# Vision tower on one core: the routed stage loads a place's expert weights in parts, without the rows that nobody reads

## What is computed

```python
def _L1_ffn_ref(hidden_states, Wg, W1, b1, W2, b2):
    x = hidden_states.reshape(-1, d)
    logits = x @ Wg
    probs = jax.nn.softmax(logits, axis=-1)
    gate = jnp.max(probs, axis=-1)
    expert_idx = jnp.argmax(probs, axis=-1)
    h = jax.nn.silu(jnp.einsum('td,edf->etf', x, W1) + b1[:, None, :])
    y = jnp.einsum('etf,efd->etd', h, W2) + b2[:, None, :]
    combine = jax.nn.one_hot(expert_idx, e, dtype=x.dtype) * gate[:, None]
    out = jnp.einsum('te,etd->td', combine, y)
```

## Time and profile before

| | |
|---|---|
| median of three executions | 3292.92 us (3288.41 to 3302.89) |
| the profiled execution's own time | 3293.8 us |
| its span | 3292.0 us |
| mean granted TensorE clock | 0.927 |
| TensorE busy | 2926.8 us (89%) |
| VectorE busy | 2119.5 us (64%) |
| loads of `w_e` | 20 of 1344 KB, median 6.4 us from issue to landing |

### The profile page before, as it was taken

How to read it: one execution, slowest core, us unless ns; L and a number is a source line. 1 busy time by engine, 2 the same in 40 slices (tenths; PEclk the granted TensorE clock), 3 DMA queues, 4 the chain that set the end, 5 groups by cost and what they waited for, 6 DMA issues and landing times. The chain is left out here.

```text
span 3292.0 us, 56595 instructions
## 1 busy us (share of the span) xinstructions
PE 2926.8 (89%) x19969; PEld 2685.5 (82%) x19969; DVE 2119.5 (64%) x5372; ACT 1109.3 (34%) x2263; POOL 608.1 (18%) x734
## 2 busy tenths in 40 slices
PE   7979999999999999999969896978969799695677
PEld 6759999999999999999968886656858699583567
DVE  2657777777777677777757773234466667785666
ACT  2433333333333233333233333114444333243333
POOL 1111221221221221221221110211223112120320
PEclk8989999999999999999989997998979889897788
DMA  3010000000000000000000000650000100000000
GB/s 128 1 51 18 35 34 34 34 18 33 34 34 34 34 17 34 34 34 34 0 36 2 1 2 5 229 195 3 1 10 18 51 18 1 10 2 3 13 18 16
DMA packets 19244, 107.77 MB, mean 33 GB/s; under 512 B 3861, under 2 KB 8869, under 8 KB 11178
## 3 DMA queue, kind: packets, MB, share of 16 engines
q1 hardware_dynamic: 17434, 101.81, 8.6%
q0 software_dynamic: 1584, 3.30, 0.3%
HBM read 100.50 MB, written 6.64 MB: 33 GB/s over the span
## 5 line engine op out<-in xcount | busy, mean ns | idle before, releaser
L766 ACT ACTIVATE hid<-bank,dat 128x384 f32<-128x384 f32 (+1 forms) x912 | 554.2, 608 | 1151.8 <-PE bank L484 1042.2
L735 PE MATMUL bank<-w,hid_hi 128*128 128x384 f32 x2964 | 848.8, 358 | 0.0
L737 PE MATMUL bank<-w,hid_lo 128*128 128x192 f32 x2964 | 742.0, 250 | 0.0
L737 PEld LDWEIGHTS bank<-w,hid_lo 128*128 128x128 f32 x2964 | 565.7, 191 | 1.7
L798 DVE TENSOR_TENSOR hid_lo<-hid,hid_hi 128x384 fp32r<-128x384 f32 (+1 forms) x912 | 539.8, 592 | 31.5
L735 PEld LDWEIGHTS bank<-w,hid_hi 128*128 128x128 f32 x2964 | 556.4, 188 | 1.8
L795 DVE CAST hid_hi<-hid 128x384 fp32r<-128x384 f32 (+1 forms) x912 | 341.0, 374 | 145.4 <-ACT hid L766 143.5
L484 PE MATMUL bank<-xa_hi,w_hi 128*128 128x384 f32 (+1 forms) x912 | 328.0, 360 | 8.6 <-DVEq L2018 8.6
L809 DVE SCALAR_TENSOR_TENSOR h_tok<-bank,gate,h_tok 128x192 f32<-128x192 f32 x416 | 173.2, 416 | 245.9 <-PE bank L737 240.9
L484 PE MATMUL bank<-xb,w_hi 128*128 128x384 f32 (+1 forms) x912 | 325.4, 357 | 0.0
L484 PE MATMUL bank<-xb,w_lo 128*128 128x384 f32 (+1 forms) x912 | 325.2, 357 | 0.0
(11 more groups left out here) (352 smaller groups left out, 4587.4 us busy)
## 6 DMA issues: line engine op xcount, KB each, us to landing
raw<-in_L_exp SPq DMA_DIRECT2D x36, 1344.0 KB, 5.7
w_e<-in_L_exp SPq DMA_DIRECT2D x20, 1344.0 KB, 6.4
pix<-in_pixels SPq DMA_DIRECT2D x6, 832.0 KB, 9.2
wp_raw<-in_L_att SPq DMA_DIRECT2D x1, 2880.0 KB, 9.9
raw<-in_L_mlp SPq DMA_DIRECT2D x2, 1344.0 KB, 5.9
route_rows<-in_rows_clear SPq DMA_DIRECT2D x1, 2000.0 KB, 22.2
x_in<-route_rows SPq DMA_DIRECT2D x5, 400.0 KB, 9.4
wp_raw<-in_L_att SPq DMA_DIRECT2D x2, 768.0 KB, 4.5
```

What stands on the lines that cost most here:

```text
L735: nc.tensor.matmul(o[:, 0:2 * D], hid_hi[k % 2][:, m, c], w2[j][:, m, :], start=m == 0, stop=False)
L737: ins = nc.tensor.matmul(o[:, 0:D], hid_lo[k % 2][:, m, c], w2[j][:, m, 0:D], start=False, stop=m == HC - 1)
L766: nc.scalar.activation(hid[(6 * k + m) % 3][:, 0:128 * nt], bank[4 + (6 * k + m) % 4][:, 0:128 * nt], func, bias=bias).then_inc(s["h_act"] ...
```

## The change

A place's load becomes three DMAs with two counters. The up part is 128 rows of 768 floats and 65 rows of 768 floats, both counted by `w_up_in`; the down part is 128 rows of 1152 floats, counted by `w_down_in`. Each part looks up the expert anew. From place 4 on the up part of a buffer is reloaded once `up` of the place before in it is done (`up_full`), the down part once `down` of that place is (`y_full`). `up` waits for 32 of `w_up_in`, `down` in addition for 16 of `w_down_in`.

```diff
-        w_e_in = [ctx.enter_context(nc.semaphore(f"w_e_in{j}")) for j in range(4)]
+        w_up_in = [ctx.enter_context(nc.semaphore(f"w_up_in{j}")) for j in range(4)]
+        w_down_in = [ctx.enter_context(nc.semaphore(f"w_down_in{j}")) for j in range(4)]
...
-                def weights(p):
+                def of_expert(p):
                     e = sp.value_load(place[0:1, p:p + 1], min_val=0, max_val=E - 1)
-                    sp.dma_start(w_e[p % 4][:, :], pack[bass.ds(e, 1)].rearrange("o p n -> p (o n)"))\
-                        .then_inc(w_e_in[p % 4], 16)
+                    return pack[bass.ds(e, 1)].rearrange("o p n -> p (o n)")
+
+                def up_weights(p):
+
+                    w, src = w_e[p % 4], of_expert(p)
+                    sp.dma_start(w[:, 0:HID], src[:, 0:HID]).then_inc(w_up_in[p % 4], 16)
+                    sp.dma_start(w[0:DB + 1, HID:2 * HID], src[0:DB + 1, HID:2 * HID]).then_inc(w_up_in[p % 4], 16)
+
+                def down_weights(p):
+                    w, src = w_e[p % 4], of_expert(p)
+                    sp.dma_start(w[:, 2 * HID:RAW], src[:, 2 * HID:RAW]).then_inc(w_down_in[p % 4], 16)
                 for p in range(3):
-                    weights(p)
+                    up_weights(p)
+                    down_weights(p)
...
                     if q == 0:
-                        weights(3)
+                        up_weights(3)
+                        down_weights(3)
+
                 for p in range(4, N):
+                    for ahead in range(p if p == 4 else p + 2, min(p + 3, N)):
+                        sp.wait_ge(route["up_full"], 2 * (ahead - 4) + 2)
+                        up_weights(ahead)
                     sp.wait_ge(route["y_full"], p - 3)
-                    weights(p)
+                    down_weights(p)
...
                 def up(p):
-                    pe.wait_ge(w_e_in[p % 4], 16 * (p // 4 + 1))
+                    pe.wait_ge(w_up_in[p % 4], 32 * (p // 4 + 1))
...
                 def down(p):
+                    pe.wait_ge(w_down_in[p % 4], 16 * (p // 4 + 1))
                     if p >= 1:
                         pe.wait_ge(route["y_kept"], p)
```

## The result

The changed kernel takes 3281.93 us (median of 15 executions, 3274.67 to 3290.34), the kernel before 3297.17 us (15 executions, 3288.41 to 3307.18) in the same measurement. The ratio is 0.9954, with a 95% interval of 0.9945 to 0.9964. That is 15.2 us; the prediction was a gain of 14.8 us and a ratio of 0.9955. The time lies inside the range of 3269 to 3290. The gain is clear of zero and, as forecast, a little under the 0.5% (16.5 us) that the prediction took as its bound for "faster".

The account below looks back on a forecast made before the run. It took TensorE and, behind it, the weight loads to bound the routed stretch. 15.95 us excess less 0.85 for the clock and 0.3 for small waits gave a 14.8 us gain: 3278.1 us, ratio 0.9955, range 3269 to 3290.

Parts of the forecast that it names:

- The sum: Routed stage: 15.95 less 0.85 for the clock and 0.3 for extra waits and the start, a gain of 14.8 us.
- the free pace: Step of TensorE's routed loop without a wait: 5.42 us, sixteen of them 86.72 us against 102.67 us.
- path: Time from a weight buffer's release to the landing of its next load; 6.87 us in the kernel before.
- cover: Time from a weight buffer's release until TensorE is ready to read it again; 5.64 us before, 19.1 us for up after.
- more than the sum: Rival: waits may be longer in some executions than in the profile, a gain of 18 to 22 us; chance 15%.
- all of it comes from one fact: Waits of `up` for `w_e` arise because its buffer is refilled only after `down(p-4)`; removal gains 15.95 us at most.
- Half clock: After the 2.72 us wait before `up(6)`, TensorE's lower clock cost 1.7 us; half counted as lost gain, 0.85 us.
- Fewer bytes: 63 of 128 rows of a place's second part not loaded, 14% fewer bytes; worth nothing beside the long cover.
- the forecast share: DMA engines' busy share in the routed stretch after the change: up to about 0.7.
- a sign against the prediction: Routed loop: SyncE issuing a down part over 3 us after its release would show the prediction wrong.
- The extra wait on TensorE: `down` waits for three semaphores in place of two: 0 for each of 20, at most 0.05 us each, 1 us in all.
- The slower rival: The 65-row load runs on too few DMA engines; if on one, 11.3 us a place, about 3370 us; chance 4%.

Follow-up runs that it names:

- the two orders: Kernel before with each place's load split into up and down DMAs with own semaphores, late release: up first, ratio 0.9948; down first, 1.0008.
- fewer bytes alone: Kernel before with a place loaded by the change's three DMAs (65 rows in the second), but one semaphore and all released by down(p-4): ratio 1.0006.
- the down part first: Kernel before with two 128-row loads per place, own semaphores, both released by down(p-4), down columns issued ahead of up columns: ratio 1.0008.
- own semaphore alone: Kernel before with two 128-row loads per place, up columns first, each with its own semaphore, both released by down(p-4): ratio 0.9948.
- all rows: Kernel after with the second up load back at all 128 rows, semaphores and reload order unchanged: ratio 0.9939.

## Why the prediction was right, and where not

**The size and its mechanism.** The sum had 15.95 us as the excess over the free pace of 5.42 us a step; the loop became 15.96 us shorter. The path of 6.87 us against a cover of 5.64 us, the reading on which the sum rests, holds: in the kernels above the wait came and went with that difference, on both sides. Path 5.4 gives almost no wait, 7.1 brings it back (the two orders), 4.9 none, and a cover of 2.7 us gives a wait in nearly every step.

**The luck in it.** That the medians differ by 15.2 us, 0.4 from the forecast, is luck: the same two kernels were 24.0 us apart when they were run again, which is beyond the 18 to 22 us of the rival "more than the sum". Both profiles of the kernel after have the loop at 86.65 us, so it is the 15.96 us of the loop that bear the forecast out, and not the third decimal of a ratio.

**What took the gain there.** Here the prediction put it wrongly. It said that "all of it comes from one fact", the refill after `down(p-4)`, and gave the gain to the early release. The runs show that the early release is enough but not needed. Loading the up columns first and waiting for them alone, with the buffer released as late as before, gives 14.7 us of the 16.0; early release with one counter in effect gives 15.9. Together they give 16.0, so the second adds about 1 us to the first. Either waiting behind `down(p-4)` for the up part alone (own counter, up part first) or taking the up part out of that load (early release with one counter) is enough, since each shortens the path below 5.64 us. The step that failed is the one that compared only the new cover of 19.1 us with the old path, and never the old cover with the new path.

**Half clock.** Between the two profiles the whole 1.7 us came back: the clock is 1.00 for the whole stretch after. The prediction gave back only half of it, in case the long wait of 2.72 us was an accident of one execution. Two runs speak against an accident. Where the path is as long as before (fewer bytes alone, and the down part first), the same step, from `down(3)` to `down(4)`, has the longest wait again, 1.96 and 2.30 us, and takes 9.18 and 10.11 us at a granted clock of 0.83 and 0.78. Whether the executions that were not profiled had it is not known, and the medians' 15.2 us fit with either. The prediction's reading that the fall goes with the longest wait holds for the profile before, but not in general: 1.76 us left the clock at 1.00 and 1.77 us did not, both in the run with fewer bytes alone.

**Fewer bytes.** Off the path they are worth nothing, as forecast. On it the prediction let them shorten the path by 14% of the transfer, and it left out the third issue: alone they made the loop no shorter (105.85 us against 102.67). The size of the DMA load was off too: the forecast share was "up to about 0.7", measured 0.77, and 0.80 in the steady step shown above. By that step a place took 0.80 x 5.42 = 4.3 us of all engines' time after; by the earlier trace rows it took 0.65 x 102.67 / 16 = 4.2 us before, for all of its bytes. The prediction had 3.2 to 3.4 plus 0.3 us. It took the rate of rows of 10,752 bytes for the new rows. By the shares and rates of the 16 steps, 1 MB took 2.9 us of all engines' time before, 2.9 with rows of 6,144 and 4,608 bytes (own semaphore alone), and 3.3 with rows of 3,072 and 4,608 bytes (all rows). So the dearer loads are those with rows of 3,072 bytes; whether it is their length or that there are three loads in place of two was not separated. A place still fits in its step, so that it cost nothing.

**Issues and the extra wait.** SyncE issues the down part 2.8 us after the first up load of its pass and 1.1 us after its release, under the 3 us that would have been a sign against the prediction; the bound of 3.3 us for a place's issues was not reached in the steady steps. The extra wait on TensorE costs 0 (steps of 5.42 us). At the start there was no wait at `up(4)`.

**The slower rival.** It was given 4% by a row of a 48-row load. With 67 rows the kernel behaves as this rival says, and the count of 65 is what keeps it away.

**What stays open.** Between the two measurements of the kernel after (0.9954 and 0.9927) there is more than their intervals explain. The rest of the program outside the loop differs by up to 17 us from profile to profile, 12 us of it already when the stage issues its first weight load; why the earlier stages differ is not known.

## What to carry to other kernels

Before restructuring when a buffer is released, compare path with cover for the bytes that the waiting instruction reads: if they are part of a larger load, issue them first and give them their own counter. Here a few lines gave 14.7 of 16 us. Moving the release earlier gave as much by itself (15.9 us), but on top of the first only about 1 us, for the landings that were then still late.

Count the rows of a load before cutting it to what is read. From 128 to 65 rows nothing was gained, and with 67 the kernel lost 2.8%.

## What the runs showed of the hardware

With a load of 67 rows in place of 65, a place took 11.0 us in place of 5.42, and the down part behind it landed after 21.1 us in place of 4.0. By the estimate above, that is one engine at about 24 GB/s.

Loads in rows of 3,072 and 4,608 bytes took 3.3 us of all engines' time for 1 MB, loads in rows of 10,752 bytes, or of 6,144 and 4,608, took 2.9. Two issues in a row stand 0.5 us apart on SyncE when no lookup lies between them.

Waits of 1.1 to 1.5 us at every second step left the granted clock at 1.00 in the kernel before. Between 1.8 and 2.7 us it varied: 1.77, 2.18, 2.30 and 2.72 us were followed by matmuls at the lower clock, 1.91 and 2.36 us were not. A wait in nearly every step, most of 1.8 to 2.4 us, brought the clock to 0.85 over 134 us.
